# Normalising the fourth layer's first batches inside the third layer's last turn, with thinner edge tables and later softmax totals

## What is computed

```python
h = jnp.maximum(_layernorm(x, axis=-1), 0.0)
x = x + _L2_gnn_ref(h, L2_gnn_W, adj, L2_gnn_bias)
h = jnp.maximum(_layernorm(x, axis=-1), 0.0)
x = x + _L3_gnn_ref(h, L3_gnn_W_lin, L3_gnn_W_val, L3_gnn_a, L3_gnn_W_out, adj, L3_gnn_src, L3_gnn_dst)
# third layer (L2_gnn)
h = jnp.einsum('bjf,kfo->kbjo', x, W)
out = adj_0 @ h[0] + adj_1 @ h[1] + adj_2 @ h[2] + bias       # diagonal, upper, lower part
# fourth layer (L3_gnn): attention over E = 256 edges, 4 heads
e = einsum('behd,hd->beh', leaky_relu(Xq[:, src] + Xq[:, dst]), a) + log(A0[src, dst] + EPS)
m = segment_max(e_t, src);  ex = exp(e_t - m[src]);  denom = segment_sum(ex, src)
Y = segment_sum((ex / denom[src])[..., None] * Vt, src)
return Y @ W_out.T
```

## Time and profile before

| | |
|---|---|
| median of 3 runs | 1212.2 us (1212.15 to 1212.97) |
| the profiled execution: its time | 1211.68 us |
| its span in the trace | 1209.7 us |
| TensorE busy (matmul / weight load) | 1162.7 us (96%) / 1022.8 us (85%) |
| VectorE, ScalarE, GpSimd busy | 987.7 us (82%), 810.7 us (67%), 410.9 us (34%) |
| third stage | 804.4 to 945.1 us |
| fourth stage, first loop / second loop | 945.4 to about 1084 us / to the end |

### The profile page before, as it was taken

How to read it: one execution, slowest core, us unless ns; L and a number is a source line. 1 busy time by engine, 2 the same in 40 slices (tenths; PEclk the granted TensorE clock), 3 DMA queues, 4 the chain that set the end, 5 groups by cost and what they waited for, 6 DMA issues and landing times. The chain is left out here.

```text
span 1209.7 us, 23745 instructions
## 1 busy us (share of the span) xinstructions
PE 1162.7 (96%) x7820; PEld 1022.8 (85%) x7820; DVE 987.7 (82%) x2735; ACT 810.7 (67%) x1810; POOL 410.9 (34%) x789
## 2 busy tenths in 40 slices
PE   5999999999999999999997999989999799999998
PEld 4798898998988989889896888877777688978997
DVE  5888988889889888898887999987777578876655
ACT  4785876858868678687685777767776467662332
POOL 4211100101001001010012777756666688853332
PEclk8999999999999999999998999999999899999999
DMA  8400000000000000000000000000000000002222
GB/s 258 121 1 1 1 2 0 0 0 0 0 0 0 0 0 0 0 0 1 1 1 1 2 1 2 2 1 1 1 1 1 1 2 2 2 1 62 71 75 74
DMA packets 26305, 20.83 MB, mean 17 GB/s; under 512 B 1776, under 2 KB 22256, under 8 KB 26224
## 3 DMA queue, kind: packets, MB, share of 16 engines
q1 hardware_dynamic: 25648, 19.68, 5.6%
q10 hardware_dynamic: 576, 0.13, 0.1%
HBM read 11.42 MB, written 8.39 MB: 16 GB/s over the span
## 5 line engine op out<-in xcount | busy, mean ns | idle before, releaser
L554 ACT ACTIVATE gate<-ps,b_lstm 128x256 f32<-128x256 f32 (+2 forms) x624 | 309.4, 564 | 94.4 <-PE ps L581 92.9
L579 PE MATMUL ps<-H_hi,w_hi 128*128 128x256 f32 (+2 forms) x624 | 210.0, 338 | 1.9 <-DVE H_lo L470 1.2
L580 PE MATMUL ps<-H_hi,w_lo 128*128 128x256 f32 (+2 forms) x624 | 204.8, 329 | 0.0
L581 PE MATMUL ps<-H_lo,w_hi 128*128 128x256 f32 (+2 forms) x624 | 192.8, 330 | 0.0
L131 POOL TENSOR_SCALAR rstd<-mv 128x8 f32<-128x8 f32 x16 | 5.0, 311 | 498.9 <-DVE mv L111 498.7
L579 PEld LDWEIGHTS ps<-H_hi,w_hi 128*128 128x128 f32 x624 | 117.6, 188 | 15.9 <-DVE H_lo L470 3.2
L580 PEld LDWEIGHTS ps<-H_hi,w_lo 128*128 128x128 f32 x624 | 117.7, 189 | 8.1
L581 PEld LDWEIGHTS ps<-H_lo,w_hi 128*128 128x128 f32 x624 | 115.3, 188 | 10.1 <-DVE H_lo L508 1.6
L579 PE MATMUL ps<-hid_hi,w_hi 128*128 128x256 f32 (+2 forms) x384 | 120.4, 320 | 0.3
L580 PE MATMUL ps<-hid_hi,w_lo 128*128 128x256 f32 (+2 forms) x384 | 116.7, 310 | 0.0
L561 ACT ACTIVATE tanh_c<-cell 128x512 f32<-128x512 f32 (+2 forms) x176 | 90.9, 517 | 24.5 <-DVE cell L498 17.4
(11 more groups left out here) (205 smaller groups left out, 3101.3 us busy)
## 6 DMA issues: line engine op xcount, KB each, us to landing
out<-x SPq DMA_DIRECT2D x32, 256.0 KB, 2.3
x<-in_WihT SPq DMA_DIRECT2D x1, 768.0 KB, 11.4
x<-in_WhhT SPq DMA_DIRECT2D x1, 768.0 KB, 6.0
x<-in_x_in SPq DMA_DIRECT2D x2, 256.0 KB, 3.7
x<-in_x_in SPq DMA_DIRECT2D x1, 512.0 KB, 8.0
x<-in_WihT SPq DMA_DIRECT2D x1, 256.0 KB, 8.3
tanh_c<-in_WqkvT SPq DMA_DIRECT2D x1, 192.0 KB, 4.8
w_sb<-in_W SPq DMA_DIRECT2D x1, 192.0 KB, 4.0
```

The lines of the kernel that those rows point to most:

```text
L554: nc.scalar.activation(gate[:, g, z, 0:w * GB], gate_bank(g, k, m)[:, 0:w * GB], ACT.Tanh if z == G else ACT.Sigmoid, bias=b_lstm[:, 4 * ( ...
L579: nc.tensor.matmul(dst, w_hi[:, src, p - 1, z], v_hi, start=start, stop=False)
L580: return nc.tensor.matmul(dst, w_lo[:, src, p - 1, z], v_hi, start=False, stop=False)
L581: return nc.tensor.matmul(dst, w_hi[:, src, p - 1, z], v_lo, start=False, stop=stop)
```

## The change

There are four edits.

1. The steps STATS2, SCALE2 and APPLY2 of the third stage also run in the last turn. `turn_start(8)` is 0, so that turn normalises batches 0 to 15 for the fourth stage and leaves them in `hn`. The fourth stage's own norm starts with group 4: no `norm_sums` stand ahead of its loop, and `transpose(0)` to `transpose(3)` wait for nothing but the block's start.
2. In the fourth stage L1114 and L1115 move from GpSimd to VectorE. They become `norm_scales(n+3)` at the end of VectorE's round, behind the softmax steps.
3. The edge tables run one operation a round (with two one-column memsets beside one of them) in rounds 0 to 13 of the third stage, behind STATS2, and VectorE waits only where an operation reads an earlier one.
4. SUMS is cut in two: FORWARD (the addition and first scan) and BACKWARD (the second scan) one round later, which puts LESS, EXPS, TURN and TAKE one round later too. TOTAL moves from n = 16, 24, 32, 40 to n = 29, 33, 41, 49 and reciprocal and product to the round behind each.

```diff
-                    elif what == SCALE2 and more:
+                    elif what == SCALE2:
...
-                    elif what == STATS2 and more:
-                        norm_stats((i + 1) * NB + g * QB, 0, QB, S["c_stats"], g * QB)
+                    elif what == STATS2:
+                        norm_stats(turn_start(i + 1) + g * QB, 0, QB, S["c_stats"], g * QB)
                         wait_apart(dve, S["c_stats"], count * QB + QB)
                         if before:
                             wait_apart(dve, S["c_shift"], count - W1 + 1)
                         norm_aggr(g * QB, QB, S["c_aggr"])
+                        edge_tables(count)
...
-                    elif what == APPLY2 and more:
+                    elif what == APPLY2:
...
-        SUMS, LESS, EXPS, TURN, TAKE, TOTAL, SHARES = range(3, 10)
+        FORWARD, BACKWARD, LESS, EXPS, TURN, TAKE = range(3, 9)
+        TOTAL_AT = [NG - 3] + [NG + 1 + k * PER for k in range(BH - 1)]
...
-                for n in range(NG):
+                for n in range(W1, NG):
                     r, sh = rstd[:, slots(n)], shift[:, slots(n)]
-                    pool.wait_ge(S["d_aggr"], n * QB + QB)
-                    nc.gpsimd.tensor_scalar(r, mv[:, slots(n), 1], EPS, None, ALU.add).then_inc(S["d_var"], 1)
-                    nc.gpsimd.tensor_scalar(sh, mv[:, slots(n), 0], -1.0, None, ALU.mult).then_inc(S["d_nmean"], 1)
...
+                    done = n - W1 + 1
+                    pool.wait_ge(S["d_var"], done)
                     nc.gpsimd.tensor_tensor(r, r, half[:, 0:QB], ALU.pow).then_inc(S["d_rstd"], 1)
...
+                def norm_scales(n):
+                    dve.wait_ge(S["d_aggr"], (n - W1 + 1) * QB)
+                    if n >= 2 * W1:
+                        dve.wait_ge(S["d_hn"], (n - 2 * W1 + 1) * QB)
+                    nc.vector.tensor_scalar(rstd[:, slots(n)], mv[:, slots(n), 1], EPS, None, ALU.add).then_inc(
+                        S["d_var"], 1)
+                    nc.vector.tensor_scalar(shift[:, slots(n)], mv[:, slots(n), 0], -1.0, None, ALU.mult).then_inc(
+                        S["d_nmean"], 1)
...
-                for n in range(3):
-                    norm_sums(n)
                 for n in range(NG):
...
-                    if n + 3 < NG:
+                    if W1 <= n + 3 < NG:
                         norm_sums(n + 3)
...
                     softmax(n)
+                    if W1 <= n + 3 < NG:
+                        norm_scales(n + 3)
```

More of the change, by code:

```diff
@@ new lines, in edge_tables @@
+                        nc.vector.memset(cut_f[:, 0:1], CUT).then_inc(S["c_table"], 1)
+                        nc.vector.memset(cut_b[:, E - 1:E], CUT).then_inc(S["c_table"], 1)
+                    elif n == 6:
+                        dve.wait_ge(S["c_table"], 8)
+                        nc.vector.tensor_scalar(cut_f[:, 1:E], changes[:, 1:E], CUT, None, ALU.mult).then_inc(
+                            S["c_table"], 1)
+                    elif n == 7:
+                        dve.wait_ge(S["c_table"], 9)
+                        nc.vector.tensor_copy(cut_b[:, 0:E - 1], cut_f[:, 1:E]).then_inc(S["c_table"], 1)
+                    elif n < 8 + 3 * EC:
+                        c, which = divmod(n - 8, 3)
+                        to, row, col = ((hot_sT[:, c], iota_e[:, 0:P], 0), (hot_dT[:, c], iota_e[:, 0:P], 1),
+                                        (same[:, c], srt[:, 0], 0))[which]
+                        nc.vector.tensor_scalar(to, row, srt_col[:, col, c:c + 1], None, ALU.is_equal).then_inc(
+                            S["c_table"], 1)
@@ L950, in stage @@
                 def stage(i, what, g, more, before):
-                    if what == STATS2 and isinstance(i, int) and i in (0, TURNS - 1):
-                        edge_tables(g if i == 0 else W1 + g)
                     count = i * W1 + g
@@ L1092, in four_layers @@
         BURST = 4
-        SUMS, LESS, EXPS, TURN, TAKE, TOTAL, SHARES = range(3, 10)
+        FORWARD, BACKWARD, LESS, EXPS, TURN, TAKE = range(3, 9)
+        TOTAL_AT = [NG - 3] + [NG + 1 + k * PER for k in range(BH - 1)]
         def due(n, what):
-            k, after = divmod(n - PER - what, PER)
-            return k if 0 <= k < BH and after == 0 else None
+            k, later = divmod(n - PER - what, PER)
+            return k if 0 <= k < BH and later == 0 else None
         with nc.Block() as block:
@@ L1153, in softmax @@
                             S["e_fb"], 1)
+                    k = due(n, BACKWARD)
+                    if k is not None:
                         if k > 0:
@@ L1171, in softmax @@
                                     S["e_ex"], 1)
-                    k = due(n, SHARES)
-                    if k is not None:
+                    if n - 1 in TOTAL_AT:
+                        k = TOTAL_AT.index(n - 1)
                         dve.wait_ge(S["e_denp"], k + 1)
```

73 lines of the change are left out of this document (32 added, 41 removed).

## The result

The changed kernel takes **1202.1 us** (median of four runs, 1201.17 to 1202.41) against 1212.2 for the kernel before (1211.98 to 1212.97, four runs on the same chip): ratio 0.9914, interval 0.9902 to 0.9926. The forecast was 1201.8. The profiled execution took 1202.18 us with a span of 1200.4, against 1211.68 and 1209.7.

The account below looks back on a forecast made before the run. TensorE paces the third stage, then idles 6.29 us for `hn` and restarts at low clock; TensorE, VectorE and GpSimd run neck and neck in the fourth's first loop. 5.15 + 1.8 + 1.8 + 0.6 + 0.5 = 9.85, so 1201.8 us, range 1199.3 to 1207.5.

Parts of the forecast that it names:

- The start: Fourth stage's first transpose needs only the block's start, with groups 0 to 3 ready in `hn`: -5.15 us.
- The clock: First to second transpose of the fourth stage runs at full clock, 3.23 us instead of 5.04: -1.8 us.
- GpSimd's pace and VectorE's pair: Fourth stage's first loop: later `hn` waits go (-2.3 us), VectorE's two added operations cost TensorE 0.5: -1.8 us.
- The softmax rounds: Three lots in the fourth stage's first loop: TensorE's two waits fall from 1.33 to 1.15 us each lot: -0.6 us.
- Totals and reciprocals: Moving them in the fourth stage changes nothing: same TensorE work, and reciprocals stood ahead of gathers behind logits: zero.
- The edge tables: Third stage, one operation a round behind the sums: -0.5 us, between -2.2 (turn 0 healed) and +1.
- The sum: All terms over the third and fourth stages together save 9.85 us from 1211.68, giving 1201.8 us.
- VectorE short of time: Rival, fourth stage's first loop: VectorE's pair takes 0.65 us instead of 0.32, giving 1205.3 us; chance 0.15.
- tables paid in the third stage: Rival: ten table operations at 0.5 us are paid in full in the third stage, giving 1207.3 us; chance 0.07.
- the clock did not fall: Rival: the clock falls all the same at the fourth stage's start, giving 1203.6 us; chance 0.06.
- The slower one: Rival, fourth stage: GpSimd's `hn` holds up VectorE's pair, which then costs 1.20 us, giving 1219.4 us; chance 0.06.

Follow-up runs that it names:

- matmuls in the gap: 11 or 6 matmuls nobody reads put ahead of the fourth stage's first transpose, against the kernel start taken back: 1210.07 us (11), 1205.45 us (6).
- start taken back: Changed kernel without its first edit: last third-stage turn leaves the norm out, fourth stage norms all 32 groups; 1209.67 us, ratio 0.9964 to the kernel before.
- start and tables taken back: Changed kernel without its first and third edits, so old fourth-stage start and old edge tables; 1209.48 us, ratio 0.9971 to the kernel before.
- gathering: Changed kernel with all softmax work of lots 0 to 2 in one round each (13, 21, 29); 1198.85 us, ratio 0.9880 to the kernel before.

## Why the prediction was right, step by step

- **The start, -5.15:** measured -5.17. The block's own start is the limit, as at the stage before. The removal of the start shows it alone: T0 comes 4.7 us later behind the third stage. What the prediction did not say is that this depends on the tables: with the old ones 3.5 us of it are lost, and the clock with them.
- **The clock, -1.8:** measured -1.84 from T0 to T1. The matmuls in the gap show the cause by themselves: the idle time. Its price is not fixed, though. Behind nearly the same gap the first two rounds lost 1.8 us (the kernel before, 6.29 us idle), 2.6 (start taken back, 5.98) and 2.1 (start and tables taken back, 5.98). And that a gap of 1.5 us costs nothing held in twelve of the thirteen traces at the third stage's start; in one the clock stood at 0.70 behind it and 1.3 us went.
- **GpSimd's pace and VectorE's pair, -1.8:** measured -1.66 from T1 to T13, but the reason given was half of it. I wrote that the later waits for `hn` go because GpSimd keeps only 3.22 us a group. Either edit alone removes nearly all of them up to T13: with the pair on GpSimd the stretch takes 44.57 us thanks to the new start (one wait of 0.27 at a weight load is left), and with the old start but the pair on VectorE there is no `hn` wait behind the first. The waits were also counted twice in part. In the kernel before, the weight load and its matmul wait for the same `hn`:

```profile
977.71 0.65 PE L1322 MATMUL ps<-ident,hn 128*128 128x128 f32 x4 [0.55 <-POOL hn L1126]
977.71 0.42 PEld L1322 LDWEIGHTS ps<-ident,hn 128*128 128x128 f32 x4 [0.74 <-POOL hn L1126]
```

  The 0.7 us of the matmuls (977.71 and 993.03) lie inside the 1.6 of the weight loads, so about 1.6 us could be won and not 2.3. VectorE's round came out as forecast: its `leaky` steps at 980.70 and 984.00 are 3.30 us apart. The lateness in rounds 2 to 5 is the 0.44 and 0.30 us at 956.79 and 960.50, 0.74 where I forecast 0.5. I put it down to the pair and the edge weights together; the kernel without the pair on VectorE has it all the same.
- **The softmax rounds, -0.6:** the waits went from 0.93 + 0.40 to 0.49 + 0.45, against 0.65 + 0.50. With the totals at their old places, T13 to T31 is 1.25 us shorter than before (72.00 against 73.25), so the term is twice the forecast. What was mis-sized is the pair. I put 0.32 in every round. In a round without softmax work it is that: 0.11 us of wait for the last `mv` and 0.19 to 0.20 for the pair, held by `hn` (980.51 to 980.70). A softmax round hides the wait, and GpSimd stands idle beside the pair:

```profile
992.48 0.69 DVE L1159 TENSOR_TENSOR_SCAN w_g<-cut_f,srt 128x256 f32<-128x256 f32 x1
993.08 0.14 DVE L1139 TENSOR_SCALAR rstd<-mv 128x4 f32<-128x4 f32 x1
993.13 0.16 DVE L1141 TENSOR_SCALAR shift<-mv 128x4 f32<-128x4 f32 x1
993.21 1.28 DVE L1196 SCALAR_TENSOR_TENSOR lr<-ps,rl 128x512 f32<-128x512 f32 x2
```

  From 993.08 to 993.21 it is 0.13 us, and 0.93 - 0.6 + 0.13 = 0.46, where 0.49 was measured. In the second round the scan took longer than in the earlier trace rows, 0.84 for 0.67 us, so that one came out near the forecast.
- **Totals and reciprocals, 0:** right (0.1 us), by an experiment that I had expected to show the opposite.
- **The edge tables, -0.5:** measured -1.0 in the third stage, all of it in turn 0. The five rounds that took 23.43 us take 22.41, against 21.25 without loss, so half of the loss stays. It stands in the first of the five (5.40 us), which is as long with the old tables (5.38), so the new placing did not touch it, and what makes it is open. The added rounds cost nothing.
- **The sum, 9.85:** the parts measured 10.96 in the profiled pair, and the medians of the runs are 10.1 us apart. That the time came within half a microsecond of 1201.8 is partly luck: stages 1 and 2 took 1.66 us longer in that execution, and the start and the clock, which make up 70% of the sum, were the terms that came out.
- **The rivals:** VectorE short of time and tables paid in the third stage did not occur, and the clock did not fall. The slower one is there in its mechanism and was wrong in its price: the pair takes 0.19 us beside `hn` and 0.13 to 0.14 without it, not 1.20. The 128x2 operation that I set against it shows nothing either way. It ran from 961.48 to 961.65, and the piece of `hn` beside it from 961.15 to 961.60: it would have ended behind the piece even without a wait. That the small chance which I gave this rival on such evidence held is luck too.

What the prediction lacked is the dependence. The removals one at a time cost 7.2 + 0.8 + 6.7 + 2.7 = 17.4 us, the change as a whole brought 11. The tables' new place is worth 0.7 us with the old start (402.26 against 401.53; 1.0 in turn 0, less the clock's 0.4) and 6.7 with the new one.

## What to carry to other kernels

When a step is moved so that the next stage waits for it, look at what stands ahead of it in its engine's queue: table work that cost nothing there may now set the stage's start. Late work on a nearly full engine belongs in the round whose consumer has other work in front of it, all of it together; spreading it evenly made two small waits a lot where gathering made almost none. An idle gap on TensorE costs its length and then the clock, here 1.8 to 2.6 us behind 6 us. And when two engines exclude each other, the price is what is left of the other's instruction when yours begins: a small operation beside pieces of 0.45 us lost under 0.1 us, a table beside one instruction of 1.3 us lost 1.1.

## What the hardware showed that I had not expected

- A `tensor_scalar` of 128x128 took 0.27 us by itself and 1.35 us when it began 0.03 us behind GpSimd's 128x512 addition. The size of that price (five times the operation) was in the earlier trace rows; that the place of the tables would decide what the new start is worth was not in my sum.
- A 128x4 `tensor_scalar` of VectorE that began 0.1 us or more into a piece of GpSimd's `hn` did not end before the piece: it ended 0.02 to 0.03 us behind it, and took 0.35 us from 0.13 in, 0.24 from 0.24 in and 0.21 from 0.26 in, against 0.14 to 0.17 alone.
- The other direction also exists: GpSimd's four `hn` pieces took 2.11 us instead of 1.74 beside VectorE's softmax operations, and the backward scan's mean went from 667 to 835 ns.
- The granted clock of the new stage's first 5 us was 0.74 behind idle times of 1.41, 0.78 and 1.20 us, none as long as the 6.29 of the kernel before; behind the changed kernel's single 1.12 it was 1.00. Once in thirteen traces it was 0.70 from 805 to 810, behind idle times of 1.48 and 0.98 us that the others had too.
- Two unchanged stages ended up to 4.8 us apart from one execution to another (802.56 to 807.32), which is half of what the whole change brings.
